# First attention: two heads share a partition tile of the query operand, and score matmuls are issued in pairs from different partition halves

## The reference

```
scores = jnp.einsum('bhqd,bhkd->bhqk', q, k) / jnp.sqrt(jnp.float32(hd))
scores = jnp.where(causal[None, None], scores, -jnp.inf)
weight = jax.nn.softmax(scores, axis=-1)
out = jnp.einsum('bhqk,bhkd->bhqd', weight, v)
```

## Time and profile before

| | |
|---|---|
| median of 3 runs | 3057.51 us (3056.87 to 3062.53) |
| profiled execution, first to last instruction | 3058.1 us |
| mean granted TensorE clock | 0.910 of full |
| PE busy / DVE busy / ACT busy | 2632.3 / 1635.8 / 1102.5 us |
| first attention, first instruction to last copy | about 541 to 1596 us |
| second attention | about 2193 to 2932 us |

### The profile page before, as it was taken

How to read it: one execution, slowest core, us unless ns; L and a number is a source line. 1 busy time by engine, 2 the same in 40 slices (tenths; PEclk the granted TensorE clock), 3 DMA queues, 4 the chain that set the end, 5 groups by cost and what they waited for, 6 DMA issues and landing times. The chain is left out here.

```text
span 3058.1 us, 38773 instructions
## 1 busy us (share of the span) xinstructions
PE 2632.3 (86%) x12386; PEld 1556.7 (51%) x12386; DVE 1635.8 (53%) x3340; ACT 1102.5 (36%) x1311; POOL 129.0 (4%) x84
## 2 busy tenths in 40 slices
PE   6969999589999999999985489797289999999946
PEld 3758888245555555555434267575244444444314
DVE  4644444677777677777603234311166665666312
ACT  3422222015555565555661122121004443444420
POOL 1200000300000000000000012200110000000000
PEclk8979999559999999999997799898659999999978
DMA  4740010420202202200004100162351222220013
GB/s 156 246 145 28 30 38 0 59 31 13 41 18 34 39 9 41 42 9 12 13 15 127 48 7 1 42 149 102 124 121 30 54 69 71 70 67 16 15 70 119
DMA packets 104052, 177.62 MB, mean 58 GB/s; under 512 B 39792, under 2 KB 45680, under 8 KB 97840
## 3 DMA queue, kind: packets, MB, share of 16 engines
q1 hardware_dynamic: 100400, 162.58, 20.6%
q10 hardware_dynamic: 3456, 12.58, 1.3%
HBM read 115.24 MB, written 59.90 MB: 57 GB/s over the span
## 5 line engine op out<-in xcount | busy, mean ns | idle before, releaser
L596 ACT ACTIVATE a_ex<-a_ps_s 128x1024 f32<-128x1024 f32 x960 | 833.1, 895 | 805.5 <-PE a_ps_s L668 402.9
L710 DVE TENSOR_REDUCE a_mx_part<-a_ps 128x1 f32<-128x512 f32 x1152 | 771.8, 688 | 257.0 <-PE a_ps L613 248.1
L613 PE MATMUL a_ps<-a_k,a_q 96*128 96x512 f32 (+3 forms) x1920 | 787.9, 453 | 92.2 <-DMA a_q<-q 87.3
L613 PEld LDWEIGHTS a_ps<-a_k,a_q 96*128 96x128 f32 x1920 | 370.2, 204 | 581.7 <-DVE a_mx_part L710 329.8
L635 PE MATMUL a_ps_o<-a_ex,a_v 128*32 128x512 f32 (+7 forms) x3840 | 609.0, 549 | 23.1 <-DVE a_o L735 19.4
L663 PE MATMUL a_ps_s<-a_q,a_k 128*128 128x512 f32 (+3 forms) x1920 | 608.1, 392 | 22.3 <-DMA a_q<-m_early 13.7
L706 DVE CUSTOM_DVE_ANT_0 a_junk<-a_ps,band 128x128 f32<-128x128 f32 (+3 forms) x768 | 369.2, 486 | 214.8 <-PE a_ps L613 211.3
L663 PEld LDWEIGHTS a_ps_s<-a_q,a_k 128*128 128x128 f32 x1920 | 353.9, 194 | 119.4 <-ACT a_ex L596 45.4
L635 PEld LDWEIGHTS a_ps_o<-a_ex,a_v 128*32 128x32 f32 (+1 forms) x3840 | 114.5, 117 | 213.8 <-issue 161.1
L668 PE MATMUL a_ps_s<-block_band,block_ident 128*128 128x128 bf16 x768 | 175.2, 234 | 0.0
L110 PE MATMUL w_ps<-w_oh,w_wh 128*128 128x512 f32 x128 | 56.8, 443 | 113.9 <-DVE w_ol L1042 113.9
(11 more groups left out here) (161 smaller groups left out, 2546.5 us busy)
## 6 DMA issues: line engine op xcount, KB each, us to landing
a_q<-q SPq DMA_DIRECT2D x48, 512.0 KB, 12.3
o<-a_o SPq DMA_DIRECT2D x64, 256.0 KB, 2.4
q<-p_oh SPq DMA_DIRECT2D x32, 256.0 KB
q<-p_ol SPq DMA_DIRECT2D x32, 256.0 KB
w_o<-o SPq DMA_DIRECT2D x32, 256.0 KB
w_z<-z SPq DMA_DIRECT2D x32, 256.0 KB
v<-p_v SPq DMA_DIRECT2D x32, 256.0 KB, 3.4
a_k<-k SPq DMA_DIRECT2D x8, 1024.0 KB, 8.3
```

Source lines behind the costliest of these rows:

```text
L596: act.activation(ex[unit % NE][:, :, off:CH], ps_s[unit % 2][:, :, off:CH], ACT.Exp, scale=SCALE).then_inc(exp_done, 1)
L613: pe.matmul(ps_1[bank][:, 0:w], q_st[set_][0:96, h, i * P:(i + 1) * P], k_st[set_][0:96, h % KH, kc * CH:kc * CH + w], start=True, stop=True)\
L710: dve.tensor_reduce(out, bank, AX.X, ALU.max).then_inc(taken1, 1)
```

## The change

In a0 the four heads are laid out in two halves of the partitions (`HALVES=2`, `ROWS=64`): heads 0 and 2 take rows 0 to 49, heads 1 and 3 take rows 64 to 113, `slot_h = h // 2` in the free dimension. A half holds 48 operand rows and directly behind them the two rows of the maximum. k is written twice, once for each half. A pass 1 matmul reads 48 rows and a pass 2 matmul 50 rows (`KM`) of one half, where both read 96 and 128 rows from partition 0 before. Between the two score matmuls of a pair stand two pass 1 blocks, and `ORDER` makes the heads alternate: pass 2 head 0 (lower half), pass 1 head 1 (upper), pass 1 head 0 (lower), pass 2 head 1 (upper), then heads 2, 3, 2, 3 in the same way. All four pass 1 blocks of a step so stand before `times_v`, and all four have the same width, since `USES1` now runs over heads last. The mask matmuls of a pair stand together behind it. The clearing of whole tiles is gone: POOL sets only blocks of 32 rows to one, before the loads land on part of them. A load of a0 is 11 DMAs for 6, and the maxima go in by two DMAs for one.

In a1 (`HALVES=1`) the rows stay as they were except that pass 2 reads 98 rows for 128; its masks too stand together behind the pair, and `USES1` has the new order.

```diff
-ATTN0 = dict(HG=4, KH=1, VH=1, DH=16, VW=32, SCALE=16 ** -0.5, GROUPS=8)
-ATTN1 = dict(HG=2, KH=2, VH=2, DH=32, VW=64, SCALE=32 ** -0.5, GROUPS=8)
+ATTN0 = dict(HG=4, KH=1, VH=1, DH=16, VW=32, SCALE=16 ** -0.5, GROUPS=8, HALVES=2)
+ATTN1 = dict(HG=2, KH=2, VH=2, DH=32, VW=64, SCALE=32 ** -0.5, GROUPS=8, HALVES=1)
...
-    USES1 = [(i, h, kc) for i in range(QT) for h in range(HG) for kc in range(i // TPC + 1)]
+    HALVES = cfg["HALVES"]
+    ROWS = P // HALVES
+    KM = KC + 2
+    ONES0 = KC // 32 * 32
+    ORDER = (1, 0, 3, 2) if HALVES == 2 else (0, 1)
+    USES1 = [(i, h, kc) for i in range(QT) for kc in range(i // TPC + 1) for h in ORDER]
...
-    LOADS = 6 * 16
+    LOADS = (1 + 5 * HALVES) * 16
+    ROWS_IN = HALVES * 16
...
-        q_st = [sb(f"q{i}", [P, HG, TOK], F32R) for i in range(3)]
+        q_st = [sb(f"q{i}", [P, HG // HALVES, TOK], F32R) for i in range(3)]
...
+                for e in range(HALVES):
+                    r0 = e * ROWS
+                    q_half = q_heads.rearrange("(p e) s r n -> e s r p n", e=HALVES)[e]
+                    sp.dma_start(k_st[set_][r0:r0 + 2 * DH].bitcast(F32), k_heads.rearrange("h s r n -> (s r) h n"))\
+                        .then_inc(landed[set_], 16)
+                    for r in (0, DH):
+                        sp.dma_start(q_st[set_][r0 + r:r0 + r + DH].bitcast(F32), q_half[0]).then_inc(landed[set_], 16)
...
-                if s > 0:
-                    pool.memset(q_st[s][CLEAR0:P].bitcast(F32), 0.0).then_inc(cleared, 1)
-                pool.memset(k_st[s][CLEAR0:P].bitcast(F32), 0.0).then_inc(cleared, 1)
-                pool.wait_ge(cleared, 2 * (s + 1))
-                pool.memset(k_st[s][96:98].bitcast(F32), 1.0).then_inc(blank, 1)
+                for e in range(HALVES):
+                    last = pool.memset(k_st[s][e * ROWS + ONES0:e * ROWS + ONES0 + 32].bitcast(F32), 1.0)
+                last.then_inc(blank, 1)
...
-                pe.matmul(ps_1[bank][:, 0:w], q_st[set_][0:96, h, i * P:(i + 1) * P],
-                          k_st[set_][0:96, h % KH, kc * CH:kc * CH + w], start=True, stop=True)\
+                r0, slot_h = h % HALVES * ROWS, h // HALVES
+                pe.matmul(ps_1[bank][:, 0:w], q_st[set_][r0:r0 + KC, slot_h, i * P:(i + 1) * P],
+                          k_st[set_][r0:r0 + KC, h % KH, kc * CH:kc * CH + w], start=True, stop=True)\
...
+                        scores(pair, 0, False)
                         if pair == 0 and n == FLIP_LATE:
                             flip(base, entry, g * 2 + 2, False)
                             entry += 1
-                        if uses1:
+                        if HALVES == 2 and uses1:
+                            for _ in range(2):
+                                max_scores(base, entry, nxt, uses1.pop(0))
+                                entry += 1
+                        scores(pair, 1, True)
+                        if masked:
+                            mask(pair)
+                        if HALVES == 1 and uses1:
                             max_scores(base, entry, nxt, uses1.pop(0))
                             entry += 1
```

More of the change, by code:

```diff
@@ L509, in load @@
                 g = turn * 3 + s
-                if clearing is not None and CLEAR0 < KC:
+                if clearing is not None and ONES0 < KC:
                     sp.wait_ge(blank, clearing)
[L512 to L516, removed]
+                k_heads, q_heads = k_d[bass.ds(g * KH, KH)], q_d[bass.ds(g * HG, HG)]
                 sp.dma_start(v_st[set_][:, :, :, :].rearrange("p h t w -> p (h t w)"),
                              v_d[g]).then_inc(landed[set_], 16)
[L519 to L522, removed]
+                for e in range(HALVES):
[5 more added lines that the diff above has]
+                        sp.dma_start(q_st[set_][r0 + r:r0 + r + DH].bitcast(F32), q_half[0]).then_inc(landed[set_], 16)
+                    sp.dma_start(k_st[set_][r0 + 2 * DH:r0 + KC].bitcast(F32),
+                                 k_heads[:, 0].rearrange("h r n -> r h n")).then_inc(landed[set_], 16)
+                    sp.dma_start(q_st[set_][r0 + 2 * DH:r0 + KC].bitcast(F32), q_half[1]).then_inc(landed[set_], 16)
             def put_rows(g, set_, early, use):
@@ L573, in _ @@
             for s in range(3):
-                if s > 0:
-                    pool.memset(q_st[s][CLEAR0:P].bitcast(F32), 0.0).then_inc(cleared, 1)
-                pool.memset(k_st[s][CLEAR0:P].bitcast(F32), 0.0).then_inc(cleared, 1)
-                pool.wait_ge(cleared, 2 * (s + 1))
-                pool.memset(k_st[s][96:98].bitcast(F32), 1.0).then_inc(blank, 1)
-                pool.wait_ge(blank, s + 1)
+                for e in range(HALVES):
+                    last = pool.memset(k_st[s][e * ROWS + ONES0:e * ROWS + ONES0 + 32].bitcast(F32), 1.0)
+                last.then_inc(blank, 1)
         @block.scalar
@@ L653, in slot @@
                     if n == 0:
-                        pe.wait_ge(rows_in[0], g * 16 + (16 + DMA0))
+                        pe.wait_ge(rows_in[0], g * ROWS_IN + (ROWS_IN + DMA0))
                     if n == LATE_CHUNK_STEP:
-                        pe.wait_ge(rows_in[1], g * 16 + (16 + DMA0))
+                        pe.wait_ge(rows_in[1], g * ROWS_IN + (ROWS_IN + DMA0))
                     off = first_col(c, t)
-                    for pair in range(PAIRS):
[L659 to L670, removed]
@@ new lines, in slot, with scores @@
+                    masked = t >= TPC * c
+                    def scores(pair, h, last_of_pair):
+                        head = 2 * pair + h
+                        r0, slot_h = head % HALVES * ROWS, head // HALVES
+                        bank = ps_s[(n * PAIRS + pair) % 2]
+                        mm = pe.matmul(bank[:, h, off:CH], k_st[set_][r0:r0 + KM, head % KH, t * P:(t + 1) * P],
+                                       q_st[set_][r0:r0 + KM, slot_h, c * CH + off:(c + 1) * CH],
+                                       start=True, stop=not masked)
+                        if last_of_pair and not masked:
+                            mm.then_inc(scores2, 1)
@@ new lines, in mask @@
+                    def mask(pair):
+                        for h in range(2):
+                            mm = pe.matmul(ps_s[(n * PAIRS + pair) % 2][:, h, off:off + P], block_ident[:, :],
+                                           block_band[:, :], start=False, stop=True)
+                        mm.then_inc(scores2, 1)
+                    for pair in range(PAIRS):
+                        pe.wait_ge(exp_done, g * UNITS + (n * PAIRS + pair - 1) + EXP0)
+                        scores(pair, 0, False)
```

10 lines of the change are left out of this document (4 added, 6 removed).

## The result

| | before | after |
|---|---|---|
| median of 20 runs each, us | 3055.0 | 3066.7 |
| lowest and highest run, us | 3041.9 to 3066.2 | 3049.8 to 3092.2 |
| profiled execution's span, us | 3058.1 | 3061.0 |
| its mean granted clock | 0.910 | 0.876 |

The account below looks back on a forecast made before the run. The prediction took PE to bound the kernel, with the ring of three banks taking over after the change. Its terms, 56 + 5 + 4 + 7 - 5 = 67 us saved, gave 3057.5 - 67 = 2990 us, range 2935 to 3115.

Parts of the forecast that it names:

- The halves run side by side: First attention's score matmuls: a pair of halves takes 0.23 us fully side by side, against 0.46 one after the other.
- serial loads: Rival, chance 0.17: the two halves' loads come one after the other; full step 3.05 us, total about 3047 us.
- serial halves: Rival, chance 0.10: halves do not run side by side; full step 3.29 us, total about 3110 us.
- The ring of three banks: Pass 1's fourth block waits for the first's bank; this loop sets a full step at 2.83 us, against 2.94 before.
- The rival that it does not bind: Rival, chance 0.08: the ring does not bind, DVE does; 161 us saved in place of 56, total about 2885 us.
- A slot of 110.0 us: First attention's slots with pass 1: 110.0 us against 118.0, 8 us saved each, 56 us for seven.
- Slot 7: First attention's last slot, without pass 1: 5 us saved, between bounds of 0 and 19.
- The start: Before the first matmul: first load 7 us earlier, doubled k costs 3.5; net 4 us saved, bounds 0 and 7.
- Second attention: A pair's masks stand together: 0.05 us saved for each of 128 pairs, 7 us in all.
- I add 5: Clock term of the sum: slots that start at half clock run less work to bring it back; 5 us lost.
- The rival's price: Clock rival, chance 0.22: each 10 us fall costs 3.2 us; 32 falls make 102 us, total 3092 us.
- The rival's cause: Clock rival, chance 0.22: the clock falls because the changed PE waits for DVE in every step; total 3092 us.

Follow-up runs that it names:

- half_read: rows64, but VectorE's maximum over full pass 1 blocks reads only half of the columns; 2957.3 us, ratio 0.9675 to the kernel before.
- rows64: The changed kernel with first-attention score matmuls reading 62 rows (pass 1) and 64 (pass 2), the added ones zero in q; 3037.0 us, ratio 0.9932.
- one_half: The changed kernel with HALVES=1 in the first attention: 48 and 50 rows a matmul, no two side by side; 3791.5 us, ratio 1.2411.
- all_rows: one_half with the first attention's score matmuls reading 96 and 128 rows, filled with zeros below row 48; 3061.5 us, ratio 1.0024.
- fill1: The changed kernel with one needless couple of score matmuls before the fourth pass 1 block of each step; 3021.4 us, ratio 0.9900.
- fill2: The changed kernel with two needless couples of score matmuls before the fourth pass 1 block of each step; 3022.0 us, ratio 0.9894.
- pv_halves: The changed kernel with the product with v cut in two, two heads behind each pair; 3153.0 us, ratio 1.0302.

## Why the prediction was wrong

**The halves run side by side** (0.23 a couple): right, by the starts in the full step after. The rivals of serial loads and serial halves are out.

**The ring of three banks, 2.83 us a full step**: right to 0.01, leg by leg, and half_read shows that it is the bound. The rival that it does not bind is out.

**A slot of 110.0 us**: mis-sized. Where the clock holds, the slot takes 113.1 us (rows64, slots 2 and 5), so 4.9 saved for 8. The steps with narrow blocks are what I made too short. Here is one with 384 columns, and one masked step (rows64, slot 5, timeline of PE):

```profile
1357.45 1.06 PE L645 MATMUL a_ps_o<-a_ex,a_v 128*32 128x512 f32 x8
...
1360.20 1.06 PE L645 MATMUL a_ps_o<-a_ex,a_v 128*32 128x512 f32 x8
...
1363.24 1.06 PE L645 MATMUL a_ps_o<-a_ex,a_v 128*32 128x512 f32 x8
```

The first takes 2.75 us (1357.45 to 1360.20), where I had 2.58, since only DVE's own leg became shorter (0.62 for 0.74), and not the two with matmuls in them (0.70 and 0.43 for 0.65 and 0.44); 256 columns came out at 2.60 for 2.33, and 128 columns at 2.46 for 2.08 (1297.94 to 1300.40). A full masked step takes 3.04 (1360.20 to 1363.24) for 3.18. The other term that was too short is the step behind the end of a chunk. VectorE copies the chunk's result out there, before it takes the next maxima; I had put that copy at nothing, and had taken 0.64 off for the product of 128 columns (rows64, slot 5, timeline):

```profile
1328.80 0.43 PE L645 MATMUL a_ps_o<-a_ex,a_v 128*32 128x128 f32 x8
...
1330.04 0.68 DVE L762 COPY a_o<-a_ps_o 128x512 f32<-128x512 f32 x1
...
1331.79 1.07 PE L645 MATMUL a_ps_o<-a_ex,a_v 128*32 128x512 f32 x8
```

This step takes 2.99 us (1328.80 to 1331.79), where my terms give 2.83 - 0.64 = 2.19: the copy's 0.68 stands in the loop and is most of the difference. Seven slots at full clock are worth 7 x 4.9 = 34 us, not 56.

**Slot 7**: 79.3 us where the clock holds (rows64), 6.5 less than before; forecast 5. In the changed kernel it takes 81.6, with its clock at 0.96.

**The start**: from POOL's first instruction to PE's first matmul 24.6 us (543.65 to 568.28), 30.6 before: 6 saved for 4.

**Second attention**: its slots take 82.7 us for 83.2, 8 x 0.5 = 4 us for 7 (in this pair of traces its slot 3, with the turn of the loop, took 2.4 of them back).

**The clock, "I add 5"**: this is the step that failed. The rival's price was about right: 3.2 us for a fall of 10 us, and the runs show 0.35 for each us at half clock. Its 32 falls would have been some 320 us at half clock; it was 223, 203 more than before. 203 x 0.35 = 71 us lost, where the sum had 5. Against 34 + 6.5 + 6 + 4 = 50 us gained that leaves 20 us lost, and the measured ratio says 12 to 23.

The rival's cause was at best half of it, though. It said that PE's waits let the clock fall. one_half hardly ever waits and has 0.50; rows64 waits as long as the changed kernel and loses a third as much. The number of rows that the matmuls read is therefore a cause by itself: in one_half against all_rows, and in the changed kernel against rows64, nothing else differs in the slots but where the maxima's rows lie. The waits may be another: the kernels that kept the clock with 48 and 50 rows (fill1, fill2, pv_halves) have more matmuls, or products over all rows for twice as long, and also shorter waits. In the trace of before, pass 1 alone stood at 0.50 with PE busy 46.3 of 48 us; I had read that as waiting, and it was also a row against reading the busy share as what the clock goes by. The Trainium skill (TensorE: Matmul & The Clock Gate, Part 1: The HAM clock gate) says that the level follows how busy TensorE has been. By PE's busy share in the profile that rule would have given one_half the full clock; its trace has 0.50, the measurement decides, and here the profile's busy time does not tell the clock.

What stays open: by what measure rows and time together decide (pass 1 alone before the change, matmuls of 96 rows, had 0.50, and slots with the same matmuls had 1.00), and why a version with the same instructions stands at 1.00 in one slot and at 0.89 in another (rows64, slots 2 and 4). The runs order the versions, no more.

## What to carry to other kernels

A matmul packed into a part of the array saves time only if the clock survives it: look at the granted clock of a stretch before and after, not only at the starts of single matmuls. Where operands end short of their half or of the array, pad them with zeros to the full height: it cost TensorE nothing and took away 148 of the 203 us at half clock here. The clearing has its price at the start: in rows64 PE's first matmul came 31.1 us after POOL's first instruction, for 24.6 in the changed kernel. Where TensorE waits anyway, a needless couple of matmuls in the wait can pay (45 us here). Before reordering around a ring of buffers, walk its loop, with everything that the consumer does in it (here the copy at a chunk's end too): the place of the long instruction did not matter, only what stands between the waiting block and it.

## What the hardware showed that I had not expected

- TensorE busy 210.00 of 210 us, its score matmuls of 48 and 50 rows one at a time, stood at a clock of 0.50 through all eight slots, and the same program with score matmuls over 96 and 128 rows, the added ones zeros, at 1.00 in five of the seven slots with pass 1: 3791 us against 3061.
- Couples of matmuls over 48 to 50 rows of each half, with waits of 0.4 us a step, let the clock fall in every slot with pass 1 (0.84 to 0.91); over 62 and 64 rows with the same waits it stood at 1.00 in three slots of eight and at 0.89 to 0.98 in the others; with 48 to 50 rows and the waits filled by two needless couples it stood at 1.00 in six slots of eight.
- Products of two heads, 32 columns each, take the 1.05 us that products of four take.
